# A graph kernel whose skip projection moves from the transformer layer into the attention layer's node step

## The chip, the cores and the metric

The program runs on one core of a Trainium2 chip. Its metric is the device time of one execution in microseconds (us); lower is better. A core has five engines that run side by side and meet only at semaphores: TensorE (PE, with its weight loads shown apart as PEld), VectorE (DVE), ScalarE (ACT), GpSimd (POOL) and SyncE (SP), which here only issues DMAs.

## The reference

A graph of 6250 nodes with 256 features and 106250 edges, sorted by destination, goes through two residual parts. The first holds two graph convolutions and a linear map. The second holds a graph attention layer with 4 heads (softmax over the edges of each node), and a transformer convolution on its result `x1`:

```
x1 = prelu(segment_sum(h[src] * alpha, dst) + gat_bias, prelu1)
q = x1 @ Wq + bq;  k = x1 @ Wk + bk;  v = x1 @ Wv + bv
logits2 = einsum('ec,ec->e', q[dst], k[src]) / sqrt(256)
alpha2 = segment_softmax(logits2, dst)
out = segment_sum(v[src] * alpha2[:, None], dst)
out = out + x1 @ Wskip + bskip
x = x + prelu(out, prelu2)
```

All is fp32. The change touches the last three lines: the sum over the edges with its value bias `bv`, and the skip term `x1 @ Wskip + bskip`.

## The kernel before

The edges are padded to 832 columns of 128. A group is 16 columns (2048 edges), so there are 52 groups; every layer goes over them in order. For each column, GpSimd issues one indirect DMA that gathers 128 source rows into `G` (4 buffers, one group each). VectorE makes a 0/1 matrix `oh` (edge by destination node of a window of 128 nodes) and TensorE adds up `oh^T G` in PSUM over the 16 columns. In this data no group needs a second window: each layer has 53 node steps, one behind each group and one last.

The four large stages by time are the preparation (to about 170 us), two convolution layers (to about 2340 us), `gat_layer` (about 2343 to 3443 us) and `transformer_layer` (about 3447 to 4609 us). A barrier of all engines stands between layers. The order on each engine is the order in which the code is written; nothing is scheduled by a planner.

**gat_layer.** In iteration k, TensorE does in this order: the broadcast `psF` (L1251, which VectorE waits for with `scol`, L1100), the sum of group k-1 (`add`, L1245), the small products `psA` of 4 columns for group k+1 (L1207), three matmuls of 128x512 into `psW` that nobody reads (L1284), and then the node step of group k-1: `node_turn` transposes the node's rows `t4` (L1215), ScalarE copies them to `lt` (L1326), and `node_multiply` makes `q` (L1222 twice, and L1223, which adds a bias by a matmul with one row of ones). ScalarE copies the result out (L1332), and SP stores `t4` and `qk` (L894, L895). The loop body covers 8 groups. Each fp32 matmul shows as two records (x2).

**transformer_layer.** It runs as a pipeline of depth three: iteration k scores group k, does the softmax chain of group k-1, and adds up group k-2. Inside an iteration there are 16 slots u. In a slot TensorE does `score(u)` (L1813, into one of two PSUM banks `psA`) and `add(u)` (L1823); VectorE does `dot(u)` (L1574, the product of `psA` with the gathered rows, summed into `L`) and one 0/1 matrix (L1549). `score(u)` waits for `dot(u-2)`, so the two engines are never more than two slots apart. The first dot of each quarter (u = 0, 4, 8, 12) waits for the gathers of that quarter. GpSimd may overwrite a quarter of `G` once TensorE has added it two iterations later, so gathers can run at most about two groups ahead. Between the slots stand the pieces of the chain and of the node step of group k-2:

- VectorE divides the sums by the softmax denominator, into `an` (L1590, slot 3). Column 256 of `an` is the sum of the weights, 1 for a node with edges and 0 for one without.
- TensorE, slot 4, `node_turn`: four transposes into `psN` (L1789: `an` twice, and the node's own rows of `x1`, `own`, twice), and a transpose of column 256 into `psO` (L1790).
- ScalarE copies `psN` to `lt` (L1906) and that row to `sa` (L1907).
- TensorE, slot 8, `node_multiply`: four matmuls into `psO` (L1796, two with `wv` and two with `wsk`), and one with `sa` (its other row is ones) and `bvs` (L1797), which adds `bv` times the weight sum and `bskip`.
- VectorE, slots 11 and 12: the two halves of the prelu from `psO` (L1597, L1598) and their sum (L1603). SP then loads `own` and `xa` for the next node step, and stores.

## Time and profile before

| what | value |
|---|---|
| three runs | 4608.73, 4602.61, 4608.18 us; median 4608.18 us |
| profiled execution | 4611.11 us, of which its span is 4609.2 us |
| mean granted TensorE clock | 0.871 of full speed |
| transformer layer, 3447 to 4609 us: busy PE, DVE, ACT, POOL | 1051.5, 782.4, 319.7, 799.2 of 1162 us; clock 0.96 |
| attention layer, 2343 to 3440 us: busy PE, DVE, ACT, POOL | 996.3, 870.9, 172.9, 780.9 of 1097 us; clock 0.89 |

Busy time of an engine is the time in which some instruction of it ran, without the time in which it issued DMAs or read registers. So POOL's busy time alone does not say how full it is: between two gathers it shows 0.30 us of "issue", in which it waited for nothing that the profile shows. The clock is the share of full speed that TensorE was granted: 1.00 is 2.4 GHz and 0.50 is 1.2 GHz. A row of a timeline gives the start, the length, and in brackets the idle time of the engine before it and what ended that. Lengths of neighbouring instructions overlap; what an instruction costs in a full stream is the distance from its start to the next one's start.

### The profile page before, as it was taken

What the parts mean: (1) busy time and instruction counts of PE and PEld (TensorE: products, weight loads), DVE (VectorE), ACT (ScalarE), POOL (GpSimd) and SP (SyncE); (2) the same over time, 40 slices, a digit from 0 to 9 for tenths busy, and PEclk for the clock granted to TensorE, in tenths of its full rate; (3) what the DMA queues carried; (4) which work ended last, traced back from release to release, by engine and by line L of the source; (5) the groups of instructions that cost most, each with busy time, mean ns of one, the idle gap of its engine ahead of it and who ended that gap; (6) DMA issues with size and microseconds to landing.
All of it is one profiled execution on the core that took longest, in us unless ns stands there. A gap on an engine that the chain in (4) does not pass through costs nothing. (4 is left out here: it accounts for less than half of the span.)

```text
span 4609.2 us, 73629 instructions
## 1 busy us (share of the span) xinstructions
PE 3524.1 (76%) x14587; PEld 2499.9 (54%) x14588; DVE 2667.7 (58%) x10225; ACT 742.4 (16%) x2298; POOL 3235.1 (70%) x3404
## 2 busy tenths in 40 slices
PE   2366666666566666666679999999978899999998
PEld 2244444444344444444456666666656676676666
DVE  8544444444333433344368888887866776776765
ACT  3200000000011111111111111111112322322322
POOL 3477777777677777777677777777727777777762
PEclk7677877777788989989878898999978999999999
DMA  5544444444444444444455555555525555555552
GB/s 165 133 129 132 130 129 131 131 128 129 114 139 136 138 137 138 139 134 138 120 143 155 150 156 151 154 152 155 150 83 141 159 154 152 160 147 145 153 146 73
DMA packets 339313, 639.35 MB, mean 139 GB/s; under 512 B 85419, under 2 KB 218598, under 8 KB 338790
## 3 DMA queue, kind: packets, MB, share of 16 engines
q0 software_dynamic: 159744, 440.25, 35.8%
q1 hardware_dynamic: 159993, 180.48, 12.4%
q10 hardware_dynamic: 19056, 12.87, 1.0%
q8 instruction: 181, 2.97, 0.3%
q14 instruction: 339, 2.78, 0.2%
HBM read 569.33 MB, written 63.99 MB: 137 GB/s over the span
## 5 line engine op out<-in xcount | busy, mean ns | idle before, releaser
L582 POOL DMA_INDIRECT g_G<-t,srcI x1664 | 1587.8, 954 | 507.1 <-issue 507.1
L755 PE MATMUL g_ps<-g_G,g_oh 128*128 128x256 f32 x3328 | 1034.0, 461 | 468.9 <-DMA g_G<-t,srcI 364.4
L755 PEld LDWEIGHTS g_ps<-g_G,g_oh 128*128 128x128 f32 x3328 | 727.9, 228 | 741.0 <-issue 404.6
L1472 POOL DMA_INDIRECT g_G<-t,srcI x832 | 798.5, 960 | 287.7 <-issue 253.3
L881 POOL DMA_INDIRECT g_G<-t,srcI x832 | 806.7, 970 | 253.3 <-issue 251.5
L1813 PE MATMUL g_psA<-g_win,g_ohT 128*128 128x257 f32 x1664 | 548.1, 414 | 105.5 <-issue 46.5
L1574 DVE CUSTOM_DVE_ANT_0 g_junk<-g_G,g_psA 128x257 f32<-128x257 f32 x832 | 348.4, 419 | 288.8 <-PE g_psA L1813 265.2
L1823 PE MATMUL g_ps<-g_G,g_oh 128*128 128x257 f32 x1664 | 509.9, 390 | 0.0
L636 DVE TENSOR_SCALAR g_oh<-iota,g_relx,g_wx 128x128 f32<-128x128 f32 x1664 | 452.2, 364 | 59.1 <-PE g_ps L755 34.0
L1245 PE MATMUL g_ps<-g_Gp,g_oh 128*128 128x264 f32 x1664 | 420.5, 403 | 22.3 <-issue 19.2
L1813 PEld LDWEIGHTS g_psA<-g_win,g_ohT 128*128 128x128 f32 x1664 | 293.0, 197 | 214.9 <-DVE g_L L1574 94.7
L1245 PEld LDWEIGHTS g_ps<-g_Gp,g_oh 128*128 128x128 f32 x1664 | 313.2, 196 | 81.9 <-issue 24.1
L643 DVE TENSOR_TENSOR g_a<-g_stage,g_own 128x256 f32<-128x256 f32 x106 | 45.8, 433 | 538.6 <-ACT g_stage L800 538.6
L1823 PEld LDWEIGHTS g_ps<-g_G,g_oh 128*128 128x128 f32 x1664 | 318.5, 194 | 68.9 <-issue 23.9
L1916 ACT ACTIVATE g_oh<-g_oh,g_p 128x128 f32<-128x128 f32 x832 | 248.7, 387 | 6.4
L1549 DVE TENSOR_SCALAR g_oh<-iota,g_relx 128x128 f32<-128x128 f32 x832 | 245.1, 296 | 5.6 <-issue 5.6
L1078 DVE TENSOR_TENSOR g_Gp<-g_G,g_psP 128x1024 f32<-128x1024 f32 x208 | 239.4, 1213 | 1.7 <-ACT g_pf L1364 1.7
L1284 PE MATMUL g_psW<-rows,ident 128*128 128x512 f32 x312 | 226.9, 887 | 0.0
L1207 PE MATMUL g_psA<-g_win,g_ohT 128*128 128x4 f32 x1664 | 211.5, 264 | 8.7 <-DVE g_ohT L973 8.7
L1207 PEld LDWEIGHTS g_psA<-g_win,g_ohT 128*128 128x128 f32 x1664 | 207.0, 206 | 10.3 <-issue 9.5
L650 DVE SCALAR_TENSOR_TENSOR g_o<-g_psO,g_rec,rows 128x256 f32<-128x256 f32 x106 | 51.3, 484 | 262.3 <-DMA t<-g_t 147.7
L800 ACT ACTIVATE g_stage<-g_ps 128x256 f32<-128x256 f32 x104 | 40.0, 384 | 993.2 <-PE g_ps L755 993.2
(293 smaller groups left out, 3901.3 us busy)
## 6 DMA issues: line engine op xcount, KB each, us to landing
g_G<-t,srcI POOLq DMA_INDIRECT x3328
g_relb<-relrow SPq DMA_DIRECT2D x104, 512.0 KB
g_own<-t SPq DMA_DIRECT2D x159, 128.0 KB
t<-g_t SPq DMA_DIRECT2D x53, 132.0 KB, 2.7
g_rec<-t SPq DMA_DIRECT2D x53, 132.0 KB
g_rec<-h SPq DMA_DIRECT2D x53, 128.5 KB
x<-g_o SPq DMA_DIRECT2D x53, 128.5 KB, 2.7
g_rec<-x SPq DMA_DIRECT2D x53, 128.5 KB
```

Source lines behind the costliest of these rows:

```text
L582: pool.indirect_dma_start(G[:, b, u, :], None, table, IOA(ap=m.srcI[:, g * UW + u:g * UW + u + 1], axis=0)).then_inc(s_g[b][u // QW], 16)
L636: nc.vector.tensor_scalar(oh[:, u, :], m.iota[:], relx[:, u:u + 1], wx[:, u:u + 1], ALU.is_equal, ALU.mult).then_inc(s_oh, 1)
L755: last = nc.tensor.matmul(ps[:, 0:D], oh[:, u, :], G[:, b, u, :], start=(u == 0), stop=(u == UW - 1))
L881: pool.indirect_dma_start(G[:, b, u, :], None, m.t3, IOA(ap=m.srcI[:, g * UW + u:g * UW + u + 1], axis=0)).then_inc(s_g[b], 16)
L1207: last = nc.tensor.matmul(psA[:, u * H:u * H + H], ohT[:, u, :], win[:, b % 2, :], start=True, stop=True)
L1245: last = nc.tensor.matmul(ps[:, 0:AGW], oh[:, b1, u, :], Gp[:, b1, u, :], start=(u == 0), stop=(u == UW - 1))
L1472: pool.indirect_dma_start(G[:, b, u, :], None, m.t4, IOA(ap=m.srcI[:, g * UW + u:g * UW + u + 1], axis=0)).then_inc(s_g[b][u // QW], 16)
L1549: return nc.vector.tensor_scalar(oh[:, b % 4, u, :], m.iota[:], relx[:, b % 2, u:u + 1], None, ALU.is_equal)
L1574: nc.vector.tensor_tensor_reduce(out=junk[:, u % 2, :], in0=G[:, b, u, :], in1=psA[:, u % 2, 0:RW], scale=1.0, scalar=0.0, op0=ALU.mult, o ...
L1813: nc.tensor.matmul(psA[:, u % 2, 0:RW], ohT[:, u, :], win[:, r, :], start=True, stop=True).then_inc(s_pa, 1)
L1823: last = nc.tensor.matmul(ps[:, r, 0:RW], oh[:, b2, u, :], G[:, b2, u, :], start=(u == 0), stop=(u == UW - 1))
L1916: last = nc.scalar.activation(src[:, u, :], src[:, u, :], ACT.Copy, scale=p[:, r, u:u + 1])
```

## The change

`x1 @ Wskip + bskip` is no longer made in the transformer layer. It is made in `gat_layer`'s node step, where the transposed rows of `x1` are already in `lt`: two matmuls and a bias matmul into a PSUM bank `psK` of its own, one more ScalarE copy to `skip`, and one more store, to a new DRAM tensor `sk`. The matmuls into `psW`, which nobody reads, go from three to two. In `transformer_layer` SP loads the rows of `sk` in place of those of `t4`; TensorE makes two transposes and two matmuls in a node step; VectorE makes `base = bv * (weight sum) + skip` in slot 6 and `v = psO + base` in slot 10, and the halves now read `v`. `bv` becomes an eleventh row of `m.rows`, broadcast to all partitions in the preparation, and the memsets of `sa` and `bvs` are gone.

```diff
 def gat_layer(nc, m):
-    LD, ST, NQ = 16, 32, UW // QW
+    LD, ST, NQ = 16, 48, UW // QW
...
                 sp.dma_start(m.qk[bass.ds(start, P), :], q_[:]).then_inc(s_st, 16)
+                sp.dma_start(m.sk[bass.ds(start, P), :], skip[:]).then_inc(s_st, 16)
...
-                nc.tensor.matmul(psO[:, 0:RW], m.ones[0:1, :], m.bqk[:], start=False, stop=True).then_inc(s_prod, 1)
+                nc.tensor.matmul(psO[:, 0:RW], m.ones[0:1, :], m.bqk[:], start=False, stop=True)
+                for j in range(2):
+                    nc.tensor.matmul(psK[:, 0:D], lt[:, j, :], m.wsk[:, j, :], start=(j == 0), stop=False)
+                nc.tensor.matmul(psK[:, 0:D], m.ones[0:1, :], m.bsk[:], start=False, stop=True).then_inc(s_prod, 1)
...
-                    for j in range(3):
+                    for j in range(2):
                         nc.tensor.matmul(psW[:], m.ident[:], m.rows[:, 0:2, :], start=True, stop=True)
...
-                nc.scalar.activation(q_[:], psO[:, 0:RW], ACT.Copy).then_inc(s_res, 1)
+                nc.scalar.activation(q_[:], psO[:, 0:RW], ACT.Copy)
+                nc.scalar.activation(skip[:], psK[:, 0:D], ACT.Copy).then_inc(s_res, 1)
...
 def transformer_layer(nc, m):
-                sp.dma_start(own[:], m.t4[bass.ds(start, P), 0:D]).then_inc(s_own, 16)
+                sp.dma_start(skip[:], m.sk[bass.ds(start, P), :]).then_inc(s_own, 16)
...
+            def node_base(n):
+                dve.wait_ge(s_own, n * LD + LD)
+                dve.wait_ge(s_x1, n + 1)
+                nc.vector.scalar_tensor_tensor(base_[:], m.row("bv"), an[:, D:RW], skip[:], ALU.mult, ALU.add).then_inc(s_base, 1)
+            def node_total(n):
+                dve.wait_ge(s_base, n + 1)
+                dve.wait_ge(s_prod, n + 1)
+                nc.vector.tensor_tensor(v[:], psO[:, 0:D], base_[:], ALU.add).then_inc(s_out, 1)
...
-                nc.vector.scalar_tensor_tensor(v[:], psO[:, 0:D], 0.0, m.row("prelu2"), ALU.min, ALU.mult)
-                nc.vector.scalar_tensor_tensor(o[:], psO[:, 0:D], 0.0, xa[:], ALU.max, ALU.add).then_inc(s_out, 1)
+                nc.vector.scalar_tensor_tensor(o[:], v[:], 0.0, xa[:], ALU.max, ALU.add)
+                nc.vector.scalar_tensor_tensor(v[:], v[:], 0.0, m.row("prelu2"), ALU.min, ALU.mult).then_inc(s_out, 1)
...
+                    if agg and u == 6:
+                        node_base(n2)
+                    if agg and u == 10:
+                        node_total(n2)
...
-                for j, src in enumerate((an, an, own, own)):
-                    nc.tensor.transpose(psN[:, j * P:j * P + P], src[:, (j % 2) * P:(j % 2) * P + P], m.ident[:])
-                nc.tensor.transpose(psO[0:1, 256:256 + P], an[:, D:RW], m.ident[:]).then_inc(s_turn, 1)
+                for j in range(2):
+                    last = nc.tensor.transpose(psN[:, j * P:j * P + P], an[:, j * P:j * P + P], m.ident[:])
...
-                for j in range(4):
-                    nc.tensor.matmul(psO[:, 0:D], lt[:, j, :], (m.wv, m.wsk)[j // 2][:, j % 2, :], start=(j == 0), stop=False)
-                nc.tensor.matmul(psO[:, 0:D], sa[:], m.bvs[:], start=False, stop=True).then_inc(s_prod, 1)
+                for j in range(2):
+                    last = nc.tensor.matmul(psO[:, 0:D], lt[:, j, :], m.wv[:, j, :], start=(j == 0), stop=(j == 1))
...
-                nc.scalar.activation(lt[:].rearrange("p j e -> p (j e)"), psN[:], ACT.Copy)
-                nc.scalar.activation(sa[0:1, :], psO[0:1, 256:256 + P], ACT.Copy).then_inc(s_lt, 1)
+                nc.scalar.activation(lt[:].rearrange("p j e -> p (j e)"), psN[:, 0:D], ACT.Copy).then_inc(s_lt, 1)
```

TensorE in the attention layer's loop, from the matmuls into `psW` to the branch behind the node step, as it stands before (`psN` takes the transposes, `lt` is their copy):

```order
L1284 MATMUL g_psW<-rows,ident 128x512 x3
L1212 ISA
L1215 MATMUL g_psN<-ident,g_t4r 128x128 x2
L1222 MATMUL g_psO<-wqk,g_lt 128x257 x2
L1223 MATMUL g_psO<-bqk,ones 128x257
L1289 COMPARE_AND_BRANCH
```

and in the changed kernel, where two more rows write `psK`:

```order
L1285 MATMUL g_psW<-rows,ident 128x512 x2
L1210 ISA
L1213 MATMUL g_psN<-ident,g_t4r 128x128 x2
L1220 MATMUL g_psO<-wqk,g_lt 128x257 x2
L1221 MATMUL g_psO<-bqk,ones 128x257
L1223 MATMUL g_psK<-wsk,g_lt 128x256 x2
L1224 MATMUL g_psK<-bsk,ones 128x256
L1290 COMPARE_AND_BRANCH
```

One matmul into `psW` has gone at the head, and three matmuls have come behind the product that makes `q`.

TensorE in the transformer layer, from behind slot 7 to the score of slot 9, before (`psR` belongs to the softmax chain):

```order
L1836 MATMUL g_psR<-ident,g_In 128x1
L1837 MATMUL g_psR<-ident,g_Out 128x1
L1810 REGISTER_ALU
L1812 REGISTER_ALU
L1813 MATMUL g_psA<-g_win,g_ohT 128x257
L1823 MATMUL g_ps<-g_G,g_oh 128x257
L1796 MATMUL g_psO<-wv,g_lt 128x256 x2
L1796 MATMUL g_psO<-wsk,g_lt 128x256 x2
L1797 MATMUL g_psO<-bvs,g_sa 128x256
L1812 REGISTER_ALU
L1813 MATMUL g_psA<-g_win,g_ohT 128x257
```

and changed, where the next score follows the two products with `wv` at once:

```order
L1850 MATMUL g_psR<-ident,g_In 128x1
L1851 MATMUL g_psR<-ident,g_Out 128x1
L1824 REGISTER_ALU
L1826 REGISTER_ALU
L1827 MATMUL g_psA<-g_win,g_ohT 128x257
L1837 MATMUL g_ps<-g_G,g_oh 128x257
L1810 MATMUL g_psO<-wv,g_lt 128x256 x2
L1826 REGISTER_ALU
L1827 MATMUL g_psA<-g_win,g_ohT 128x257
```

Three matmuls have gone between `add(8)` and `score(9)`; in the same way the two transposes of `own` and L1790 have gone in slot 4.

VectorE in the transformer layer, slots 10 and 11, before (each L1574 pair is a dot):

```order
L1574 ISA g_junk,g_L<-g_G,g_psA 128x257
L1574 ISA g_L 128x1
L1549 TENSOR_SCALAR g_oh<-iota,g_relx 128x128
L1554 TENSOR_SCALAR g_ohT<-g_relb,iotap 128x512
L1712 REGISTER_ALU
L1574 ISA g_junk,g_L<-g_G,g_psA 128x257
L1574 ISA g_L 128x1
L1549 TENSOR_SCALAR g_oh<-iota,g_relx 128x128
L1593 ISA
L1594 ISA
L1597 SCALAR_TENSOR_TENSOR g_v<-g_psO,rows 128x256
L1598 SCALAR_TENSOR_TENSOR g_o<-g_psO,g_xa 128x256
```

and changed, with the sum of `psO` and `base` in slot 10:

```order
L1572 ISA g_junk,g_L<-g_G,g_psA 128x257
L1572 ISA g_L 128x1
L1547 TENSOR_SCALAR g_oh<-iota,g_relx 128x128
L1600 TENSOR_TENSOR g_v<-g_psO,g_base 128x256
L1552 TENSOR_SCALAR g_ohT<-g_relb,iotap 128x512
L1723 REGISTER_ALU
L1572 ISA g_junk,g_L<-g_G,g_psA 128x257
L1572 ISA g_L 128x1
L1547 TENSOR_SCALAR g_oh<-iota,g_relx 128x128
L1603 ISA
L1606 SCALAR_TENSOR_TENSOR g_o<-g_v,g_xa 128x256
L1607 SCALAR_TENSOR_TENSOR g_v<-g_v,rows 128x256
```

The halves stay in slot 11, in the other order, and read `v` in SBUF; one instruction has come in slot 10 and one, `base`, in slot 6.

## Rows read from the trace of the kernel before

**Rows 1.** L1472, the gathers of the transformer layer: its own times, its waits.
```profile
L1472 POOL DMA_INDIRECT g_G<-t,srcI x832: 940/946/1242, 3448.0 to 4533.1; - x167
...
  PE g_ps L1823: 34.2, 36
```

**Rows 2.** Timeline of POOL: start, length, engine, line, operation, count, idle time before it.
```profile
3502.26 0.95 POOL L1472 DMA_INDIRECT g_G<-t,srcI  x1 [0.30 <-issue]
...
4015.41 0.95 POOL L1472 DMA_INDIRECT g_G<-t,srcI  x1 [0.30 <-issue]
```

**Rows 3.** Timeline of DVE, the dot product that waits for a gather early in the layer.
```profile
3505.29 0.42 DVE L1574 CUSTOM_DVE_ANT_0 g_junk<-g_G,g_psA 128x257 f32<-128x257 f32 x1 [1.18 <-DMA g_G<-t,srcI]
```

**Rows 4.** Timeline of PE in the transformer layer, one group of edges.
```profile
3971.73 0.38 PE L1789 MATMUL g_psN<-ident,g_own 128*128 128x128 f32 x2
...
3972.05 0.60 PE L1813 MATMUL g_psA<-g_win,g_ohT 128*128 128x257 f32 x2
...
3976.79 1.03 PE L1796 MATMUL g_psO<-wsk,g_lt 128*128 128x256 f32 x4
...
3978.38 0.70 PE L1813 MATMUL g_psA<-g_win,g_ohT 128*128 128x257 f32 x2
...
3992.22 0.38 PE L1789 MATMUL g_psN<-ident,g_own 128*128 128x128 f32 x2
```

**Rows 5.** Timeline of DVE in the transformer layer, the same group.
```profile
3979.11 0.42 DVE L1574 CUSTOM_DVE_ANT_0 g_junk<-g_G,g_psA 128x257 f32<-128x257 f32 x1 [2.44 <-PE g_psA L1813]
...
3982.07 0.42 DVE L1597 SCALAR_TENSOR_TENSOR g_v<-g_psO,rows 128x256 f32<-128x256 f32 x1
3982.41 0.41 DVE L1598 SCALAR_TENSOR_TENSOR g_o<-g_psO,g_xa 128x256 f32<-128x256 f32 x1
...
3988.59 0.42 DVE L1574 CUSTOM_DVE_ANT_0 g_junk<-g_G,g_psA 128x257 f32<-128x257 f32 x1 [1.30 <-PE g_psA L1813]
```

**Rows 6.** Timeline of PE behind the jump back of the loop over eight groups.
```profile
4031.52 1.22 PE L1813 MATMUL g_psA<-g_win,g_ohT 128*128 128x257 f32 x2 [4.56 <-issue]
```

**Rows 7.** Timeline of PE in the attention layer, one group.
```profile
2763.24 4.52 PE L1284 MATMUL g_psW<-rows,ident 128*128 128x512 f32 x6
...
2767.59 0.38 PE L1215 MATMUL g_psN<-ident,g_t4r 128*128 128x128 f32 x2
2768.63 1.11 PE L1222 MATMUL g_psO<-wqk,g_lt 128*128 128x257 f32 x4 [0.66 <-ACT g_lt L1326]
2769.67 0.70 PE L1223 MATMUL g_psO<-bqk,ones 1*128 1x257 f32 x2
2770.21 0.28 PE L1251 MATMUL g_psR<-g_pf,ones 1*128 1x4 f32 x2
```

**Rows 8.** Windows there: stretch, busy of PE, PEld, DVE, ACT, POOL, granted clock, DMA, GB/s.
```profile
2763.60:2766.80 3.20, 3.20 (x5) 1.30 (x4) 2.27 (x5) 0.20 (x1) 2.48 (x3) 0.50 0.46 127
...
2767.00:2770.20 3.20, 2.54 (x10) 1.44 (x9) 3.20 (x4) 0.38 (x1) 2.59 (x3) 1.00 0.45 112
```

**Rows 9.** Waits in the attention layer, 2400 to 3300 us: total, times, longest.
```profile
DVE g_scol L1100 <- PE g_psR L1251: 22.8, 26, 2.5
...
POOL g_G L881 <- DVE g_Gp L1078: 1.8, 6, 0.3
```

**Rows 10.** Timeline of PE and SP, the last node step of the attention layer.
```profile
3438.57 2.05 PE L1222 MATMUL g_psO<-wqk,g_lt 128*128 128x257 f32 x4 [0.66 <-ACT g_lt L1326]
3440.55 1.22 PE L1223 MATMUL g_psO<-bqk,ones 1*128 1x257 f32 x2
...
3443.11 0.38 SPq L895 DMA_DIRECT2D qk<-g_q  x1
```

**Rows 11.** Timeline of DVE and PE, the end of the program.
```profile
4571.85 0.42 DVE L1574 CUSTOM_DVE_ANT_0 g_junk<-g_G,g_psA 128x257 f32<-128x257 f32 x1 [1.28 <-PE g_psA L1813]
...
4602.27 1.55 PE L1796 MATMUL g_psO<-wsk,g_lt 128*128 128x256 f32 x4
4603.75 0.70 PE L1797 MATMUL g_psO<-bvs,g_sa 33*128 33x256 f32 x2
```

More of the change, by code:

```diff
@@ L212, in _ @@
                 sp.dma_start(bqc[:], a["bq"].rearrange("(k p) -> p k", p=P)).then_inc(s_w, 16)
-            sp.wait_ge(s_set, 1)
-            for r, n in ((0, "bv"), (RB, "bskip")):
-                sp.dma_start(m.bvs[r:r + 1, :], a[n].rearrange("(a n) -> a n", a=1)).then_inc(s_w, 16)
+            sp.dma_start(m.bsk[:], a["bskip"].rearrange("(a n) -> a n", a=1)).then_inc(s_w, 16)
             sp.wait_ge(s_sums, 2)
@@ L224, in _ @@
             sp.wait_ge(s_set, 2)
-            for t_, n in ((m.t3, AGW), (m.xa, D), (m.t2, D), (m.x1, RW), (m.t4, RW), (m.qk, RW)):
+            for t_, n in ((m.t3, AGW), (m.xa, D), (m.sk, D), (m.t2, D), (m.x1, RW), (m.t4, RW), (m.qk, RW)):
                 sp.dma_start(t_[NP - P:NW, :].rearrange("(k p) n -> p k n", p=P), zrow[:, :, 0:n]).then_inc(s_st, 16)
@@ L829, in gat_layer @@
         v, v2, t4, lt, q_ = sb("v", [P, D]), sb("v2", [P, D]), sb("t4r", [P, RW]), sb("lt", [P, 2, P]), sb("q", [P, RW])
+        skip = sb("skip", [P, D])
         mx, ls, m2, ab, sm, rs = (sb(n, [P, H]) for n in ("mx", "ls", "m2", "ab", "sm", "rs"))
@@ L832, in gat_layer @@
                                        psb("psO", [P, 512]), psb("psR", [P, 512]))
-        psW = psb("psW", [P, 512])
+        psW, psK = psb("psW", [P, 512]), psb("psK", [P, 512])
         psB = psR[:, 256:256 + 2 * H].rearrange("p (j h) -> p j h", j=2)
@@ L1417, in transformer_layer @@
         run, In, Lb, Out = sb("run", [1, P + 1]), sb("In", [1, P]), sb("Lb", [1, P + 1]), sb("Out", [1, P])
-        own, xa, an, lt, sa = sb("own", [P, D]), sb("xa", [P, D]), sb("an", [P, RW]), sb("lt", [P, 4, P]), sb("sa", [RB + 1, P])
+        skip, xa, an, lt, base_ = sb("skip", [P, D]), sb("xa", [P, D]), sb("an", [P, RW]), sb("lt", [P, 2, P]), sb("base", [P, D])
         v, o, rs = sb("v", [P, D]), sb("o", [P, D]), sb("rs", [P, 1])
@@ L1428, in transformer_layer @@
          s_s2, s_cpy, s_bt, s_edge, s_W2, s_M, s_z, s_exp, s_gp, s_xch, s_xoh, s_xop, s_xpa, s_xpu, s_xwin, s_own,
-         s_sum, s_x1, s_turn, s_lt, s_prod, s_out, s_res, s_st) = (sem(n) for n in (
+         s_sum, s_x1, s_base, s_turn, s_lt, s_prod, s_out, s_res, s_st) = (sem(n) for n in (
              "zero", "relx", "oh", "hT", "pa", "pu", "aq", "ok", "agx", "ev", "scol", "pf", "F", "s1", "rt", "run", "Lb", "In",
              "s2", "cpy", "bt", "edge", "W2", "M", "z", "exp", "gp", "xch", "xoh", "xop", "xpa", "xpu", "xwin", "own",
-             "sum", "x1", "turn", "lt", "prod", "out", "res", "st"))
+             "sum", "x1", "base", "turn", "lt", "prod", "out", "res", "st"))
         block = c.enter_context(nc.Block())
@@ L1608, in node_all @@
                 node_scale(n)
+                node_base(n)
+                node_total(n)
                 node_halves(n)
@@ L1785, in node_turn @@
                 pe.wait_ge(s_x1, n + 1)
[L1786 removed]
                 hold(m, pe)
[L1788 to L1790 removed]
+                for j in range(2):
+                    last = nc.tensor.transpose(psN[:, j * P:j * P + P], an[:, j * P:j * P + P], m.ident[:])
+                last.then_inc(s_turn, 1)
             def node_multiply(n):
@@ L1794, in node_multiply @@
                 hold(m, pe)
-                for j in range(4):
-                    nc.tensor.matmul(psO[:, 0:D], lt[:, j, :], (m.wv, m.wsk)[j // 2][:, j % 2, :], start=(j == 0), stop=False)
-                nc.tensor.matmul(psO[:, 0:D], sa[:], m.bvs[:], start=False, stop=True).then_inc(s_prod, 1)
+                for j in range(2):
+                    last = nc.tensor.matmul(psO[:, 0:D], lt[:, j, :], m.wv[:, j, :], start=(j == 0), stop=(j == 1))
+                last.then_inc(s_prod, 1)
             def body(k, kq, kh, b, past):
@@ L1958, in body @@
                 return nwin, xb
[L1960 removed]
+            act.wait_ge(s_zero, 1)
             act.sem_inc(s_ev, 1)
@@ L1983, in build @@
         m.x, m.out = a["x"], out
-        m.xa, m.t1, m.t2 = (dram(n, (NW, D)) for n in ("xa", "t1", "t2"))
+        m.xa, m.t1, m.t2, m.sk = (dram(n, (NW, D)) for n in ("xa", "t1", "t2", "sk"))
         m.h0, m.x1 = dram("h0", (NW, RW)), dram("x1", (NW, RW))
```

27 lines of the change are left out of this document (11 added, 16 removed).

## The prediction

> **What bounds the kernel now.** I read the table of busy times first. In the transformer layer TensorE is busy for nine tenths of the time, but the waits decide. The rows of L1472 show the gathers: the first starts at 3448.0, the last at 4533.1, and only 34.2 us of that is waiting for TensorE to free a buffer [rows 1]. A gather takes 0.95 us and 0.30 us of issue follows it [rows 2]. Group 28 begins at 4015.41 [rows 2], so 28 groups took 567.4 us, 20.26 us each: this is GpSimd's own pace while it is little disturbed.
>
> The timelines of TensorE and VectorE show the consumers. In an even stretch a group takes 3992.22 - 3971.73 = 20.49 us [rows 4]. Over a long stretch it is more: from the dot of slot 8 of group 2 at 3505.29 [rows 3] to that of slot 15 of group 51 at 4571.85 [rows 11] are 1066.6 us for 49.4 groups, 21.57 us each. The 1.08 us above 20.49 are stalls such as the 4.56 us of issue behind the loop's jump back, which the gathers cannot make good [rows 6]. So the layer is bound by TensorE and VectorE together at 21.57 us a group, and the gathers at 20.26 are the next floor. At the end the consumers are 4571.85 - 4533.1 = 38.7 us behind the last gather.
>
> In an even stretch TensorE has no idle time to speak of in the slots and VectorE waits for it, longest for 2.44 us behind the node step's products [rows 5]. The 1.30 us before the first dot of an iteration [rows 5] I take for VectorE's own (it reads its table there, and the score was ready earlier), so it stays.
>
> In the attention layer the gathers wait 1.8 us in 900 [rows 9]: the consumers set that layer's pace too. VectorE waits there for `psF`, which TensorE reaches behind the node step, 26 times in about 43 iterations [rows 9]. What lengthens TensorE's node step there is paid where that wait occurs.
>
> **The change part by part.** *Transformer layer, TensorE.* The transposes of `own` and of the weight sum go: 3972.05 - 3971.73 = 0.32 us. The two products with `wsk` and the bias matmul go: 3978.38 - 3976.79 = 1.59 us [rows 4]. That is 1.91 us a group, all in TensorE's full stream.
>
> *Transformer layer, VectorE.* `base` and the sum come. Neither shows before; the nearest row is a half, 3982.41 - 3982.07 = 0.34 us from start to start [rows 5]. `base` in slot 6 cancels the 0.32 us won in slot 4, since VectorE is late in slots 6 to 8. The 2.44 us wait then shrinks by about 1.8 us, `dot(9)` comes that much earlier, and the sum in slot 10 takes 0.34 back. A group takes 20.49 - 1.5 = 19.0 us, with the stalls 20.1. Bounds: TensorE alone, 20.49 - 1.91 = 18.6, with the stalls 19.7; nothing given back, 21.57. I take 20.1, because the rows show VectorE with room only in that one wait. That is 0.2 us below the gathers' 20.26, so the gathers become the bound, if narrowly.
>
> *What that is worth.* At 20.26 us a group the last gather starts at 3448.0 + 52 x 20.26 - 1.25 = 4500.4, 32.7 us earlier. A gather that is waited for reaches its dot 3505.29 - 3502.26 = 3.0 us after its start [rows 2, 3]. The last quarter then has three more slots at 1.2 us. With one quarter's lag (5 us, about one stall like that of rows 6, since the consumers are hardly faster than the gathers) the last dot is at 4500.4 + 3.0 + 3.6 + 5 = 4512 in place of 4571.85: **-60 us**. The lag can be 0 (-65) or, with consumers at 20.9 us a group, some 32 us more (-28).
>
> *Its tail.* Two iterations without gathers follow; each loses 1.9 us on TensorE. The last node step loses 4603.75 - 4602.27 = 1.48 us of `wsk` [rows 11] and about 0.5 us of bias matmul, and its shorter copies pay for the added sum: **-6 us**. ScalarE's shorter copies elsewhere lie beside the slots and are worth nothing.
>
> *Attention layer, each group.* Added on TensorE: two matmuls as L1222, 2769.67 - 2768.63 = 1.04 us, and one as L1223, 2770.21 - 2769.67 = 0.54 us [rows 7]: 1.58 us. Removed: one of three into `psW`. The three take 2767.59 - 2763.24 = 4.35 us [rows 7]; most of that is at a granted clock of 0.50, 1.2 GHz, the node step behind them at 1.00 [rows 8]. A record that takes 0.87 us at half clock takes 0.43 at full; 4.35 us is four slow and two quick ones. If the two quick ones go, 0.87 us is saved; on the mean it is 1.45; if two slow ones go, 1.74. The net is between -0.16 and +0.71 us; I take +0.4 in the iterations in which VectorE waits, 26 of 43, so 0.25 x 52 = **+13 us**, with -8 and +37 as ends. The copy to `skip` and the third store (SP issues one in about 0.4 us, [rows 10]) come when ScalarE and SP have long waits of their own; their cover is gone only behind the last group.
>
> *Attention layer, end.* Nothing covers the last node step. It runs at half clock: the two `wsk` matmuls as L1222, 3440.55 - 3438.57 = 1.98 us, the bias one 1.22 us, one copy and one store issue 0.4 us each [rows 10]: **+4 us**. If TensorE were warm it would be +2.
>
> *Preparation and loads.* One more broadcast row and one bias row less, other rows of the same size in the transformer layer, a shorter start of GpSimd: 0, within 1 us either way.
>
> Sum: -60 - 6 + 13 + 4 = -49 us. The profiled execution took 4611.1 us, so 4562; the median of the runs shown is 2.9 us below that execution, which makes **4559 us**.
>
> **The rivals.** *The clock in the attention layer (slower).* The matmuls into `psW` stand behind the small products with 4 columns, after which the clock is at 0.50 though TensorE was busy throughout, and they run while it comes back to 1.00 [rows 8]. With one fewer it may stay down through the node step. L1222's pair then takes 1.98 in place of 1.04 and the bias matmul 1.22 in place of 0.54 [rows 7, 10], and both stand there twice: 2 x 0.94 + 2 x 0.68 = 3.2 us a group. It decides from 15 groups on (15 x 3.2 = 49, all the gain); in 30 groups it gives 4559 + 96 = 4655 us. For it: the third matmul is the one that ends closest to the change of level. Against it: the added matmuls are work of the same sort at the same place, and two of 512 columns still fill nearly the whole slow stretch. 9 in 100.
> The Trainium skill (Perfetto Trace Analysis, section Matmul Optimizations) speaks for this rival: it says that the matmul engine scales its power with utilization, so matmuls should run back to back in batches. The trace agrees so far as rows 8 show both levels inside one iteration; a removed matmul shortens such a batch. By that rule alone the layer would get slower; by the rows it is only open.
>
> *The two engines stay the bound.* VectorE's added 0.68 us and the slot-by-slot tie (score waits for the dot two slots back) eat more than I count, and a group stays at 20.9 us with the stalls. For it: VectorE already lags TensorE in slots 6 to 8. Against it: its longest wait is 2.44 us, more than three times what is added. Then the last dot comes 49.4 x 0.64 = 32 us later: 4591 us. 17 in 100.
>
> *The gain is given back.* The change does its work on TensorE, but the slots are in fact set by VectorE's and the semaphores' latencies, and the attention layer pays its upper end of +37: -28 + 37 = 4611 or nearly nothing. 5 in 100.
>
> *More than forecast.* The lag vanishes and the attention layer hides its part: -65 - 6 + 4 = 4541 us. 13 in 100.
>
> **How the numbers follow.** My case has 56 in 100, with its own range 4545 to 4582 (the lag and two thirds of the attention layer's bounds). The range of 8 in 10 runs from 4532 to 4598: it takes in the better case and the second rival and leaves out the clock and the worst of the third. A change of 0.2%, 9 us, is about what a measurement of this kernel can tell from none. Faster: my case, the two engines and the better one, 86 less one for their upper edges, 85; same: most of the third, 4; slower: the clock and the rest, 11.
>
> **What would show it.** After, the gathers of the transformer layer should wait for TensorE for a few us in place of 34, their last start should be near 4500 plus what the attention layer lost (some 15 us), and dots should wait for gathers all along the layer. The wait of VectorE behind the node products should be near 0.7 us, an even group 20.1 to 20.3. In the attention layer a group should be 0.1 to 0.4 us longer, and the clock 1.00 in the node step. I am wrong in the mechanism if the gathers still wait 30 us, if dots wait for TensorE as long as before, or if L1222's successor runs at half clock.

## The result and the profile after

| | before | after |
|---|---|---|
| median of the runs shown | 4607.6 us | 4665.24 us (4660.12 to 4668.71, 4 runs) |
| ratio | 1 | 1.0122, 95% interval 1.0109 to 1.0135 |
| span of the profiled execution | 4609.2 us | 4660.3 us |
| mean granted TensorE clock | 0.871 | 0.850 |

The change made the kernel 1.2% slower. I had forecast 4559 us. The miss lies in one layer. The rows of L1470, the gathers of the transformer layer after, show on which side of it (min, median and longest ns, first and last start; then what its idle time ended on and who waited for it):

```profile
L1470 POOL DMA_INDIRECT g_G<-t,srcI x832: 942/947/1210, 3570.4 to 4617.3; - x167
...
  issue: 253.4, 832
...
  DVE g_junk L1572: 34.2, 26
```

The first gather starts at 3570.4 us; before it was 3448.0 [rows 1]. So all that stands ahead of the transformer layer lost **122.4 us**. From the first to the last gather it was 1085.1 us and is 1046.9, **38.2 less**. From the last gather to the end of the span it was 76.1 us and is 43.0, **33.1 less**. 122.4 - 38.2 - 33.1 = +51.1 us, the difference of the spans. GpSimd now waits for nothing in the transformer layer (all of its idle time is issue), where it had waited 34.2 us for TensorE. VectorE waits for gathers 26 times.

The groups of that layer on TensorE, from one node step to the next:

```profile
3993.26 0.38 PE L1803 MATMUL g_psN<-ident,g_an 128*128 128x128 f32 x2
...
4013.51 0.41 PE L1803 MATMUL g_psN<-ident,g_an 128*128 128x128 f32 x2
...
4032.34 0.38 PE L1803 MATMUL g_psN<-ident,g_an 128*128 128x128 f32 x2
...
4051.05 0.38 PE L1803 MATMUL g_psN<-ident,g_an 128*128 128x128 f32 x2
```

The distances are 20.3, 18.8 and 18.7 us, where an even group took 20.49 [rows 4]. The consumers can do 18.8 and wait for the gathers in between.

The loss is in the attention layer. One row for the layer of each kernel, between the first and the last copy of `ps` to `stage` (stretch, its length, busy PE, PEld, DVE, ACT, POOL, granted clock, DMA share, GB/s), before:

```profile
2365.80:3428.40 1062.60, 973.73 (x4637) 696.31 (x4636) 851.76 (x2956) 167.86 (x608) 763.62 (x788) 0.90 0.55 146
```

and after:

```profile
2366.70:3545.00 1178.30, 1096.83 (x4840) 773.64 (x4840) 853.55 (x2956) 181.52 (x659) 764.20 (x788) 0.82 0.50 137
```

It took 1062.6 us and takes 1178.3, 115.7 more, and the clock fell from 0.90 to 0.82. At a granted clock c, TensorE does in t us what it could do in c x t at full clock. So (1 - c) x length is what it could have done more at full clock: 0.10 x 1062.6 = 106 us before, 0.18 x 1178.3 = 212 after. I call this **the clock's part**, and the remainder **the rest**: work at full clock and waits, 956 us before and 966 after. The second decimal of the clock makes each uncertain by up to 6 us, and a difference of two by some 8. The rest grew by 10 us; the clock's part grew by 106. This is bookkeeping, not yet a cause: the clock's part also counts slow time in which TensorE had nothing to do, and where another engine sets the layer's pace a lower clock costs no time at all.

TensorE's busy time grew by 1096.83 - 973.73 = 123 us, all of the layer's 116 and a little more. So the layer got longer because TensorE was at work for longer, and not because it waited for the new copy or store.
The Trainium skill (TensorE: Matmul & The Clock Gate, HAM oscillation — how this bites in real kernels) reckons the penalty of a throttled time in the same way, as that time times one less the share of the clock. No row measures the penalty by itself; two pairs of runs below that differ by the same products, and whose rests both differ by 84 us (each within 8), fit it.

The waits there, 2400 to 3300 us, after:

```profile
DVE g_scol L1098 <- PE g_psR L1252: 103.6, 39, 5.5
POOL g_G L878 <- DVE g_Gp L1076: 74.5, 27, 6.4
```

VectorE waits for `psF` 103.6 us in place of 22.8, and GpSimd for VectorE 74.5 in place of 1.8 [rows 9]. The 1.8 us say what set the pace before: gathers that practically never wait run at GpSimd's own rate. The layer's 832 gathers start from 2309.3 to 3368.1, which is 20.4 us for a group of 16, beside the 20.26 that the prediction read in the next layer. Now they start from 2309.8 to 3457.4 and wait for 98.0 us on the way: the path through TensorE and VectorE sets the pace.

Two neighbouring groups of TensorE's timeline after; the second starts at 2787.90:

```profile
2762.11 3.76 PE L1285 MATMUL g_psW<-rows,ident 128*128 128x512 f32 x4
2765.66 0.63 PE L1213 MATMUL g_psN<-ident,g_t4r 128*128 128x128 f32 x2
2766.95 2.05 PE L1220 MATMUL g_psO<-wqk,g_lt 128*128 128x257 f32 x4 [0.66 <-ACT g_lt L1327]
...
2770.08 2.08 PE L1223 MATMUL g_psK<-wsk,g_lt 128*128 128x256 f32 x4
...
2773.11 0.42 PE L1252 MATMUL g_psR<-g_pf,ones 1*128 1x4 f32 x2
...
2787.90 3.19 PE L1285 MATMUL g_psW<-rows,ident 128*128 128x512 f32 x4
2790.88 0.63 PE L1213 MATMUL g_psN<-ident,g_t4r 128*128 128x128 f32 x2
...
2795.44 0.28 PE L1252 MATMUL g_psR<-g_pf,ones 1*128 1x4 f32 x2
...
2808.82 3.62 PE L1285 MATMUL g_psW<-rows,ident 128*128 128x512 f32 x4
```

The first group takes 25.8 us, the second 20.9. In the second, `L1220` and what follows run at full clock, as before [rows 7]. From the turn to `psF` it takes 4.56 us, where it took 2770.21 - 2767.59 = 2.62 [rows 7]. In the first it takes 7.45, because the whole node step runs at half clock. The windows of the first group:

```profile
2758.00:2762.00 4.00, 4.00 (x34) 3.98 (x33) 3.35 (x17) 0.96 (x4) 3.08 (x4) 0.90 0.58 171
2762.00:2766.00 4.00, 4.00 (x8) 1.72 (x7) 3.07 (x6) 0.00 (x0) 3.08 (x4) 0.50 0.42 112
2766.00:2770.00 4.00, 3.34 (x8) 1.68 (x6) 2.78 (x4) 0.38 (x1) 2.06 (x3) 0.50 0.31 87
2770.00:2774.00 4.00, 4.00 (x10) 2.84 (x10) 0.04 (x1) 0.57 (x2) 2.97 (x4) 0.50 0.38 101
2774.00:2778.00 4.00, 4.00 (x11) 2.83 (x10) 2.85 (x14) 0.60 (x3) 3.09 (x4) 0.50 0.68 156
2778.00:2782.00 4.00, 4.00 (x19) 3.44 (x18) 3.76 (x18) 1.04 (x4) 3.08 (x4) 0.97 0.72 177
```

The clock falls to 0.50 in the small products (`L1205`, at 2761.2), with TensorE busy for 4.00 of 4.00 us, and is back only some 17 us later, in the sums of the next iteration. Before, it was back when the node step began [rows 8]. The trace after has 16 stretches of 17 us in the layer; before, the longest was 10 us and most were 3.4.

### The profile page after: what moved, and what is told of

It is laid out like the page before. It is cut to its first block and busy times, and to the rows that moved or that the text cites. A ratio compares the mean times of both kernels' runs of the same rounds, so it can differ in the third digit from the quotient of the medians.

```text
span 4660.3 us, 73367 instructions
## 1 busy us (share of the span) xinstructions
PE 3555.8 (76%) x14324; PEld 2492.7 (53%) x14325; DVE 2706.3 (58%) x10331; ACT 737.0 (16%) x2298; POOL 3230.8 (69%) x3401
## 5 line engine op out<-in xcount | busy, mean ns | idle before, releaser
L1470 POOL DMA_INDIRECT g_G<-t,srcI x832 | 794.6, 955 | 253.4 <-issue 253.4
L1246 PE MATMUL g_ps<-g_Gp,g_oh 128*128 128x264 f32 x1664 | 449.0, 422 | 12.9 <-issue 12.9
L1246 PEld LDWEIGHTS g_ps<-g_Gp,g_oh 128*128 128x128 f32 x1664 | 331.0, 207 | 78.1 <-issue 13.2
L1837 PEld LDWEIGHTS g_ps<-g_G,g_oh 128*128 128x128 f32 x1664 | 315.3, 192 | 66.3 <-issue 22.8
L1547 DVE TENSOR_SCALAR g_oh<-iota,g_relx 128x128 f32<-128x128 f32 x832 | 243.7, 295 | 1.2 <-issue 1.2
L1205 PE MATMUL g_psA<-g_win,g_ohT 128*128 128x4 f32 x1664 | 212.8, 264 | 10.6 <-DMA g_win<-t 10.6
L1205 PEld LDWEIGHTS g_psA<-g_win,g_ohT 128*128 128x128 f32 x1664 | 208.3, 207 | 12.2 <-issue 11.3
L965 DVE TENSOR_SCALAR g_oh<-iota,g_relx 128x128 f32<-128x128 f32 x832 | 173.5, 297 | 24.6 <-PE g_ps L1246 16.7
```

What stands on the lines that cost most here:

```text
L1205: last = nc.tensor.matmul(psA[:, u * H:u * H + H], ohT[:, u, :], win[:, b % 2, :], start=True, stop=True)
L1246: last = nc.tensor.matmul(ps[:, 0:AGW], oh[:, b1, u, :], Gp[:, b1, u, :], start=(u == 0), stop=(u == UW - 1))
L1470: pool.indirect_dma_start(G[:, b, u, :], None, m.t4, IOA(ap=m.srcI[:, g * UW + u:g * UW + u + 1], axis=0)).then_inc(s_g[b][u // QW], 16)
L1547: return nc.vector.tensor_scalar(oh[:, b % 4, u, :], m.iota[:], relx[:, b % 2, u:u + 1], None, ALU.is_equal)
L1837: last = nc.tensor.matmul(ps[:, r, 0:RW], oh[:, b2, u, :], G[:, b2, u, :], start=(u == 0), stop=(u == UW - 1))
```

## The experiments

Each ratio is to runs of the kernel before, taken beside them on the same chip. For each kernel I give the layer's length and split it as above. Fillers are the matmuls into `psW`. A length comes from one profiled execution, which lay between 10 us under and 7 us over the median of its kernel, so differences of less than some 15 us between two layers are not read. The stretch runs from the first to the last copy of `ps` to `stage` each time; the row stands with its experiment.

| kernel | skip products | matmuls into `psW` | layer | clock's part | rest |
|---|---|---|---|---|---|
| before | none | 3 | 1062.6 | 106 | 956 |
| e2 | none | 2 | 1062.7 | 181 | 882 |
| e3 | none | 3 | 1054.4 | 105 | 949 |
| after | in the node step | 2 | 1178.3 | 212 | 966 |
| e1 | in the node step | 3 | 1201.2 | 168 | 1033 |
| g8 | in the node step | 0 | 1216.9 | 353 | 864 |
| e4 | in the node step, `psF` ahead of it | 2 | 1129.0 | 169 | 960 |
| g5 | behind `psF`, one iteration late | 2 | 1139.7 | 205 | 935 |
| g7 | as g5, and `psF` ahead | 2 | 1172.3 | 223 | 950 |
| h1 | ahead of `psW`, one iteration late | 2 | 1230.6 | 271 | 960 |

**e3: the transformer layer's part alone.** The node step of the attention layer is as before, with three matmuls into `psW`; ScalarE's result `q` is stored to `sk` in place of the skip term, so the output lacks that term. The store and all of the transformer layer are those of the change.

```diff
-                nc.tensor.matmul(psO[:, 0:RW], m.ones[0:1, :], m.bqk[:], start=False, stop=True)
-                for j in range(2):
-                    nc.tensor.matmul(psK[:, 0:D], lt[:, j, :], m.wsk[:, j, :], start=(j == 0), stop=False)
-                nc.tensor.matmul(psK[:, 0:D], m.ones[0:1, :], m.bsk[:], start=False, stop=True).then_inc(s_prod, 1)
+                nc.tensor.matmul(psO[:, 0:RW], m.ones[0:1, :], m.bqk[:], start=False, stop=True).then_inc(s_prod, 1)
```

> The changed transformer layer with the attention layer's node step as before: three matmuls into psW, no products with wsk there; what is stored as the skip rows is a copy of q, so the output lacks the skip term. Theory (the transformer layer's part is worth what its own rows show, about 70 us, and all of the loss is in the attention layer's TensorE work): 4608 - 70 = 4538 us, with up to 4 more for the third store, and the layer's gathers never wait for TensorE. Rival (part of those 70 us came from the longer attention layer, which left the transformer layer's first loads or phase in a better place): 4550 to 4575 us.

```profile
2364.30:3418.70 1054.40, 967.57 (x4634) 691.77 (x4634) 851.24 (x2956) 167.79 (x608) 762.32 (x788) 0.90 0.55 153
```

Measured: 4530.9 us, ratio 0.9833 (0.9816 to 0.9851), 73 us faster than before. Of these, 8 us are in the attention layer, within its spread, and about 65 behind it, where 66 were forecast. So the third store and the transformer layer's change cost nothing and bring what was forecast; the loss is in the products and the copy of the attention layer.

**e2: the kernel before with two matmuls into `psW`.**

```diff
-                    for j in range(3):
+                    for j in range(2):
```

> The kernel before with two matmuls into psW in place of three, nothing else. Theory (the number of these matmuls decides): long stretches at 0.50 appear as in the changed kernel, some 10 to 16 of them at about 5 us each, and the saved matmul gives back at most 0.9 us in the other groups: 4608 + 70 - 35, about 4640 us, and at least 4615. Rival (the longer node step is needed for it): no long stretch, the layer loses 0 to 0.9 us a group: 4565 to 4608 us.

```profile
2361.30:3424.00 1062.70, 979.17 (x4535) 709.72 (x4535) 854.27 (x2956) 167.82 (x607) 763.78 (x788) 0.83 0.53 146
```

and of its waits, 2400 to 3300 us:

```profile
POOL g_G L881 <- DVE g_Gp L1078: 0.9, 3, 0.3
```

Measured: 4603.6 us, ratio 1.000 (0.999 to 1.001). The rest fell by 74 us and the clock's part rose by 75. Taking the third matmul out of the kernel before gives nothing. The equal length by itself does not say that the clock ate the saving, though: the gathers wait for 0.9 us in 900, so they set this layer's pace with two fillers as with three, and at an equal length the split has to balance. The busy time says more: TensorE is busy for 979.17 us in place of 973.73, with 102 matmul records fewer. So the clock took back what the matmul had cost, and the gathers would have hidden a gain in any case. The theory's time (at least 4615 us) was missed. Its stretches came nonetheless: the trace has 15 of 10 us, three of 14 and two of 17, and 17 us was the longest. They cost nothing here.

**e1: the changed kernel with three.** The edit of e2 turned round.

> The changed kernel with three matmuls into psW, as before. Theory (the third matmul keeps TensorE's clock up through the node step): the 16 long stretches at 0.50 of the attention layer go to none or one; each group pays 0.9 to 1.4 us more for the matmul than a quick group does now (21.2 to about 22.2 us), and the layer comes out near 52 x 22.2 plus its loop stalls, some 40 us shorter than in the changed kernel: about 4620 us. Rival (the clock stays down because the node step itself grew, whatever stands ahead of it): the long stretches stay, and the layer gets 45 to 75 us longer: 4710 to 4740 us.

```profile
2364.20:3565.40 1201.20, 1110.53 (x4936) 781.58 (x4936) 850.83 (x2956) 181.48 (x659) 761.97 (x786) 0.86 0.48 134
```

Measured: 4677.01 us, ratio 1.0147 (1.0129 to 1.0165). This lies between the two numbers expected. The long stretches are gone, 42 of 56 now last 7 us and the others 3.4, and the clock's part is 44 us less, but the rest is 67 more. So the missing third matmul is not the cause of the loss. Put back, it makes the profiled layer 23 us longer and the median 12 us; the intervals of the two ratios touch, so it helps nothing and may cost a little. Against e3, which differs by the skip products and their copy alone, e1 has 84 us more of rest (1.6 us a group, all of the 1.58 that I had read for the added matmuls) and 63 more of the clock's part: 147 us. TensorE's busy time makes up 1110.53 - 967.57 = 143 of them, so the products cost this, and not the copy. With two into `psW` (e2 against after) the same products cost 84 of rest and 31 of clock: 116 us.

**g8: the changed kernel with none.** The loop of matmuls into `psW` is taken out.

> The changed kernel with no matmul into psW. If the fillers are only load (theory B, and the reading that the third one of e1_three cost 12 us), the group loses 2 to 3 us of TensorE's work: attention layer 1080 to 1130 us, 4580 to 4630. If they keep the clock up, the stretches at the lower clock grow and the layer stays at 1178 or above: 4665 to 4720.

```profile
2361.50:3578.40 1216.90, 1107.65 (x4631) 818.33 (x4630) 858.64 (x2956) 181.57 (x659) 764.61 (x787) 0.71 0.49 133
```

Measured: 4701.83 us, ratio 1.0219 (1.0187 to 1.0251). The rest falls by 102 us and the clock's part grows by 141; nearly every group now has a stretch of 14 us and takes 23.9 us. Two fillers are worth their time here, some 40 us of it, and the third is not; a single one was not run.
The Trainium skill (Perfetto Trace Analysis, Matmul Optimizations) asks for matmuls back to back in batches because the engine's power goes by utilization. For the clock these runs agree: with none, two and three fillers the layer's clock is 0.71, 0.82 and 0.86. For the time they agree only from none to two.

**e4: `psF` ahead of the node step.** TensorE makes the broadcast before `node_turn`, in the same iteration, and not behind the node step.

```diff
-                if agg:
-                    pe.wait_ge(s_exp, k)
-                    hold(m, pe)
-                    nc.tensor.matmul(psF, m.ones[0:1, :], pf[:], start=True, stop=True).then_inc(s_pf, 1)
...
+                if logits:
+                    pe.wait_ge(s_exp, k + 1)
+                    hold(m, pe)
+                    nc.tensor.matmul(psF, m.ones[0:1, :], pf[:], start=True, stop=True).then_inc(s_pf, 1)
                 if agg:
                     node_turn(n1)
```

> The changed kernel with the broadcast psF made ahead of the node step in the same iteration, so that VectorE's scol does not wait for the node step. Theory (the added 1.9 us of the node step reach the group time through that wait, 104 us in 39 groups): VectorE's wait for psF goes below 5 us, quick groups fall from 21.2 to 20.4 or so and slow ones from 25.8 to about 24: some 50 us less, 4615 us. Rival (TensorE itself is full from one end of the iteration to the other, and the wait only shows it): VectorE's wait moves to another product of TensorE and the time stays within 15 us of 4665.

```profile
2362.00:3491.00 1129.00, 1075.18 (x4837) 741.00 (x4837) 854.69 (x2956) 181.69 (x659) 764.92 (x788) 0.85 0.51 143
```

and its waits, 2400 to 3300 us:

```profile
POOL g_G L878 <- DVE g_Gp L1076: 45.9, 16, 6.8
DVE g_oh L965 <- PE g_ps L1246: 40.7, 47, 1.7
```

Measured: 4616.45 us, ratio 1.0024 (1.0012 to 1.0036), 49 us faster than the changed kernel. The wait for `psF` is gone, and VectorE waits for the sums instead. The theory's number, 4615 us, came out. In the split the gain is 43 us of clock and 6 of rest: the same work in another order drew one stretch of 17 us in place of 16, and seven of 14 in place of one. By the rows of the two windows TensorE is busy for 22 us less and idle for 28 less (53.8 in place of 81.5). So both the shorter wait and the clock may have part in the 49 us, and this run does not divide them.

**g5: the skip products behind `psF`.** They are made one iteration late, behind the first quarter of the next sums, from the `lt` that is still there; the copies of `q` and `skip` follow them.

```diff
                 if agg:
                     add(0)
+                    node_skip()
```

> The same kernel as in the run on moving the skip products behind psF, on another chip. If the kernel before shows groups of 20.0 to 20.5 us there: theory A (the distance from the node step's turn to psF sets the group) expects quick groups of 20.0 to 20.5, the wait of DVE for psF back at some 25 us in all, and 4560 to 4600 us; theory B (all of TensorE's work in an iteration sets it) expects groups of 21 us and more and 4640 to 4670. If the kernel before shows groups near 34 us, neither is tested.

```profile
2361.40:3501.10 1139.70, 1075.67 (x4841) 784.43 (x4841) 855.25 (x2956) 181.30 (x658) 763.22 (x788) 0.82 0.53 142
```
```profile
DVE g_scol L1099 <- PE g_psR L1255: 46.8, 30, 4.2
```

Measured: 4627.96 us, ratio 1.0059 (1.0037 to 1.0081). The distance from turn to `psF` is that of before, the wait for `psF` is half, and the quickest groups are 19.6 to 20.2 us. The layer gains 39 us, 31 of them rest, which I put down to the shorter path. The clock's part is unchanged within its uncertainty. Neither theory's number was met: the time lies between them.

**g7: both moves.**

> Both moves: psF ahead of the node step and the skip products behind it, two matmuls into psW. With groups of 20.0 to 20.5 us in the kernel before: theory A expects the attention layer back at 1055 to 1075 us and 4535 to 4570; theory B expects it between 1110 and 1150 and 4600 to 4640, since TensorE's work is that of the changed kernel.

```profile
2366.50:3538.80 1172.30, 1104.45 (x4835) 781.34 (x4834) 857.56 (x2956) 181.47 (x659) 763.21 (x787) 0.81 0.51 138
```

Measured: 4655.82 us, ratio 1.0111 (1.0076 to 1.0146). The two gains of 49 and 39 us do not add; together they give 6. The clock's part is 54 us above that of e4. The theory that the distance to `psF` sets the group fell here.

**h1: the skip products in the filler's place.** They are made one iteration late, directly ahead of the two matmuls into `psW`, and the copy and the store of `skip` lag by one step. Nothing is left out.

```diff
+                if agg:
+                    if not (isinstance(k, int) and k == 1):
+                        pe.wait_ge(s_res, n1)
+                        hold(m, pe)
+                    node_skip()
                 if logits:
                     for j in range(2):
                         nc.tensor.matmul(psW[:], m.ident[:], m.rows[:, 0:2, :], start=True, stop=True)
```

> The skip products of a node step are made one iteration later, directly ahead of the two matmuls into psW, where before stood a third one; the copy to skip and its store follow one iteration late. TensorE's stream is then like the one before the change (1.7 us of skip products in place of a filler of 1.45), and the way from the node step's turn to psF is as short as before. Theory P (place: it was the longer way to psF and the clock inside the node step that cost): attention layer 1055 to 1080 us, stretches at the lower clock mostly of the shortest kind, 4535 to 4565 us in all, faster than both kernels. Theory L (load: any more work of TensorE in this layer costs its time and brings the clock down): attention layer 1110 to 1180, 4590 to 4665.

```profile
2365.20:3595.80 1230.60, 1144.81 (x4841) 800.10 (x4842) 853.52 (x2956) 182.44 (x658) 764.18 (x788) 0.78 0.47 132
```
```profile
3024.03 5.40 PE L1213 MATMUL g_psA<-g_win,g_ohT 128*128 128x4 f32 x32
3029.29 2.05 PE L1233 MATMUL g_psK<-wsk,g_lt 128*128 128x256 f32 x4
3031.27 1.22 PE L1234 MATMUL g_psK<-bsk,ones 1*128 1x256 f32 x2
3032.42 3.77 PE L1302 MATMUL g_psW<-rows,ident 128*128 128x512 f32 x4
3036.00 0.41 PE L1221 MATMUL g_psN<-ident,g_t4r 128*128 128x128 f32 x2
```
```profile
3024.00:3028.00 4.00, 4.00 (x28) 3.98 (x28) 3.35 (x18) 0.79 (x4) 3.08 (x4) 0.72 0.59 186
3028.00:3032.00 4.00, 4.00 (x13) 2.94 (x13) 3.07 (x6) 0.17 (x1) 2.04 (x3) 0.50 0.41 114
3032.00:3036.00 4.00, 4.00 (x7) 1.41 (x6) 2.99 (x4) 0.00 (x0) 0.93 (x1) 0.50 0.00 0
3036.00:3040.00 4.00, 3.25 (x16) 2.41 (x15) 0.22 (x1) 1.04 (x3) 2.85 (x4) 1.00 0.38 103
```

Measured: 4712.23 us, ratio 1.0229 (1.0204 to 1.0253), slower than the changed kernel, where the one theory had expected the fastest of all. The rest is that of the changed kernel. The clock's part is 59 us more: in this group the clock is already down in the small products, stays down through the skip products and the fillers, and is back when the node step multiplies. The theory of the place fell. That of load expected at most 4665 us, so its time was missed too; only the rest behaves as it says.

**h2: the value bias alone.** The kernel before, with nothing changed but the bias: VectorE makes `base = bv * (weight sum) + bskip` in slot 6 and adds it in slot 10; TensorE keeps the products with `wsk` and loses the fifth transpose and the bias matmul. It computes all of the reference.

```diff
+                nc.vector.scalar_tensor_tensor(base_[:], m.row("bv"), an[:, D:RW], m.row("bskip"), ALU.mult, ALU.add).then_inc(s_base, 1)
...
-                nc.tensor.transpose(psO[0:1, 256:256 + P], an[:, D:RW], m.ident[:]).then_inc(s_turn, 1)
...
-                nc.tensor.matmul(psO[:, 0:D], sa[:], m.bvs[:], start=False, stop=True).then_inc(s_prod, 1)
```

> The kernel before with only the value bias changed: VectorE adds bv times the weight sum and the skip bias (one scalar_tensor_tensor and one sum more), TensorE makes neither the bias matmul nor the fifth transpose in the transformer layer; the skip products stay there. The attention layer is that of the kernel before: 1055 to 1070 us. In the transformer layer TensorE loses about 0.6 us a group and VectorE gains 0.68: if TensorE sets the groups, an even group is 19.9 to 20.3 and the layer 1050 to 1070, 4575 to 4595 in all; if VectorE sets them, nothing or a loss, 4600 to 4625.

```profile
2365.30:3429.00 1063.70, 973.14 (x4628) 697.96 (x4628) 850.99 (x2956) 167.65 (x608) 762.20 (x788) 0.90 0.53 146
```
```profile
L1464 POOL DMA_INDIRECT g_G<-t,srcI x832: 940/946/1191, 3448.4 to 4512.6; - x167
...
  PE g_ps L1832: 20.0, 8
```
```profile
3964.19 0.38 PE L1798 MATMUL g_psN<-ident,g_an 128*128 128x128 f32 x2
...
3984.09 0.38 PE L1798 MATMUL g_psN<-ident,g_an 128*128 128x128 f32 x2
...
4004.08 0.38 PE L1798 MATMUL g_psN<-ident,g_an 128*128 128x128 f32 x2
```

Measured: **4579.42 us**, ratio 0.993 (0.9913 to 0.9947): 29 us faster than before, and it beats both kernels. The attention layer is untouched. In the transformer layer a group takes 19.9 and 20.0 us in place of 20.49, and from the first gather to the last are 1064.2 us, 20.9 less. About 0.6 us of TensorE's work for 0.7 of VectorE's was a good trade, since TensorE set the groups there.

**Nine runs in which the kernel before took 6146 to 6191 us.** On three occasions every kernel took a third longer, the one before too. One chip of these gave 4608 us for the kernel before on a later occasion, so it is not the chip as such. These are the edits of e5 (as g5), e6 (g5 with three into `psW`), e7 (as g7), e8 (as g8) on one chip, f5, f7, f8 (again as g5, g7, g8) and f9 (g7 with none into `psW`) on another, and i1 on a third. i1 is e3 with the one-row bias matmul into `psK` more, without the two big products. Of the expectations I quote those that no other run repeats:

> As the run before, with three matmuls into psW. Theory A: the third matmul adds its 0.9 to 1.7 us to the path up to psF again, as it did in the run with three (23.6 us a group there, with the clock down for two units in place of one): 20 to 50 us more than with two, 4625 to 4655 us. Rival (with the products out of the way the third matmul is hidden, as it is in the kernel before, where two and three give the same time): within 10 us of the run with two.

> Both moves and no matmul into psW. Theory C: with psF off the path a low clock in the node step delays nobody but TensorE itself, which has 3 us less to do: quick and slow groups both near VectorE's own 20.2 us, 4608 - 73 + 10, about 4545 us. Rival D: the clock stays down through the sums as well (about 4 us more for a group's sums alone), groups of 23 us or more: above 4650 us.

> The run with the changed transformer layer alone (three fillers, attention layer 1054 us, 4531 in all), and in its attention node step only the one-row bias matmul into psK more (0.69 us at full clock, 1.22 at half); the two big skip products are left out, and the output lacks the skip term. In proportion to TensorE's time (theory L): 0.4 of the 147 us that the whole projection cost with three fillers, attention layer near 1113, 4575 to 4605. Only the longer way to psF: 0.7 to 1.2 us in half of the groups, 1070 to 1085, 4545 to 4565. A jump (any addition tips the clock): 1150 and more, 4620 and more. Nothing: 1050 to 1060, 4525 to 4540.

| kernel | time, us | ratio, 95% interval |
|---|---|---|
| e5, e6 | 6140.19, 6142.44 | 0.9986 (0.9975 to 0.9997), 0.9989 (0.9977 to 1.0001) |
| e7, e8 | 6123.56, 6134.8 | 0.9972 (0.9958 to 0.9985), 0.9986 (0.9972 to 0.9999) |
| f5, f7 | 6205.4, 6200.55 | 1.0023 (1.0008 to 1.0038), 1.0013 (1.0002 to 1.0024) |
| f8, f9 | 6210.67, 6195.3 | 1.0034 (1.0018 to 1.005), 1.0005 (0.9993 to 1.0016) |
| i1 | 6175.1 | 0.999 (0.9977 to 1.0004) |

TensorE in the attention layer of f5:

```profile
3401.57 0.61 PE L1206 MATMUL g_psA<-g_win,g_ohT 128*128 128x4 f32 x4
3403.97 0.17 PE L1206 MATMUL g_psA<-g_win,g_ohT 128*128 128x4 f32 x1 [1.79 <-issue]
3406.14 0.17 PE L1206 MATMUL g_psA<-g_win,g_ohT 128*128 128x4 f32 x1 [2.00 <-issue]
3408.99 0.17 PE L1206 MATMUL g_psA<-g_win,g_ohT 128*128 128x4 f32 x1 [2.68 <-issue]
```

Between single small matmuls TensorE stands still for 1.8 to 2.7 us with nothing to wait for that the profile shows. A group takes about 34 us, against which 1.6 us of products are little. All nine lie within 0.35% of the kernel before and tell the theories apart in nothing. What e6 and i1 were to show is open.

## Why the prediction was wrong

**The transformer layer: right.** I forecast the gathers as the new bound and their last start 32.7 us earlier within the layer, for -60 and -6 us in all. Behind the last gather that left 60 + 6 - 32.7 = 33.3 us. Measured: 38.2 and 33.1, 71.3 us in all against 66. The wait for TensorE is gone, dots wait for gathers, and between such waits a group runs at 18.7 or 18.8 us where I had added up 19.0.

**The attention layer's end: right.** Between the last eviction there and the first of the next layer it was 86.2 us and is 90.8, +4.6 against +4.

**The attention layer, each group: wrong.** The step that failed is "I take +0.4 in the iterations in which VectorE waits, 26 of 43, so 0.25 x 52 = +13 us". Measured: +115.7. It rests on a misreading that stands earlier: "the gathers wait 1.8 us in 900 [rows 9]: the consumers set that layer's pace too". Gathers that do not wait set the pace themselves. So less work on TensorE could gain nothing there, and more work than the gathers left room for had to cost in full. The sum also netted two things, and both were read at a clock that stays as it is. The rest did grow by only 10 us, near the forecast +13, but that is luck: it is 84 for the products less 74 that e2 shows to be worth no time. Both price and clock came out otherwise:

- The removed matmul was credited with 0.87 to 1.74 us a group. e2 shows it worth 0: the gathers hold the length, and TensorE's busy time did not fall either, because its clock did.
- The added products were priced at 1.58 us. e3 against e1 and e2 against after show that in full, 84 us of rest both times, without cover on the mean of the 52 groups, and 31 to 63 us of clock on top. I had also thought that only the 26 of 43 iterations with a wait would pay.

So the sum from the runs is 0 + 84 + 31 = 115. The sign that the prediction had set for a wrong mechanism, L1222's successor at half clock, came in about every third group.

**The rival I gave 9 in 100** was the clock in this layer, and it is what came: 16 long stretches, each group with one 4.6 us above its neighbours, and 4665 us where I had written 4655 for 30 groups. That the two times lie so near is luck: 16 stretches of 4.6 us make 74 us and not 96, and the other groups are slower too, 20.8 to 21.9 us in the main. Its mechanism was half right. I had it decide by the missing third matmul, and priced it as the node step alone at half clock, 3.2 us. The stretch also covers the first sums of the next iteration, hence 4.6. e1 shows that the third matmul removes these stretches and still does not bring the time back; e2 shows that without the skip products they cost nothing.

**The argument I used against that rival** ("the added matmuls are work of the same sort at the same place") did not hold: rows 8 showed that the level changes inside the group with TensorE busy throughout. A level that changes while the engine stays busy cannot be taken as fixed to a place, and I should have given the clock a third of the chances and an upper end of 80 us or more.

**A sum of the third rival** does not close: with -28 and +37 the others of its terms, -6 and +4, give +7 us on 4608, so 4615 and not 4611. Nothing hangs on it.

**What stays open:** why the same matmuls in another order give 169, 205, 212, 223 or 271 us of clock's part. No run here names a rule that orders e4, g5, after, g7 and h1. Of the guesses on record, the two for g7 missed their ranges by 16 and 86 us, the two for h1 by 47 and 147.

## What to carry to other kernels

Look first at which engine never waits: it sets the pace, work taken off another one gains nothing, and work added there costs as soon as its slack is used up. Where the granted clock changes level inside a loop, split a layer's time into what the clock takes and the rest, and forecast the two apart; the second can be summed from rows, the first has to be run. Filler matmuls beside such a drop are neither free nor sure savings: test their number at both ends before crediting one. Do an edit's parts apart: the part that moved no work into the full engine kept four tenths of the gain (29 of 73 us) at none of the loss.

## What the runs showed of the hardware that I had not expected

- The clock went to 0.50 with TensorE busy for 4.00 of 4.00 us, in products with 4 columns, and stayed there for some 17 us of fp32 matmuls, most of them 128x512, 128x257 and 128x264, without a gap above 0.66 us.
- The mean clock of the same layer moved with a few matmuls a group and with their order: 0.90 and 0.83 with three and two fillers and no skip products, 0.86, 0.82 and 0.71 with three, two and none beside the skip products, 0.78 with the skip products ahead of two fillers.
- On some occasions the whole program takes a third longer (6146 to 6191 us in place of 4604 to 4608), with gaps of 2 us between single matmuls, and kernels that differ by 1 to 2% elsewhere lie within 0.35% of the kernel before there.
